# Rope on even and odd tiles, and a later place for its high and low halves, in the attention of a three-part layer

## What is computed

```python
def rotate_half(x):
    x1 = x[..., ::2]
    x2 = x[..., 1::2]
    return jnp.stack((-x2, x1), axis=-1).reshape(x.shape)

qkv = x @ Wqkv.T                     # x is layer-normalised before
q, k, v = split and turned to (b, head, t, 16)
q = cos * q + rotate_half(q) * sin   # angles: one frequency for each pair of features
k = cos * k + rotate_half(k) * sin
scores = q k^T / sqrt(16), causal
out = softmax(scores) v, heads side by side, @ Wo.T

x = x + 0.5 * ffn(layernorm(x))
x = x + attention(layernorm(x))
x = x + 0.5 * ffn(layernorm(x))
```

## Time and profile before

| | us |
|---|---|
| median of three timed runs | 2371.58 |
| their range | 2366.81 to 2373.09 |
| the profiled execution | 2371.06 |
| its span, from first to last instruction | 2369.3 |

### The profile page before, as it was taken

The page is one execution under the profiler, slowest core; times in us unless marked ns, Lnnn a source line. Parts: engine busy times, 40 slices in busy tenths (PEclk is TensorE's granted clock), DMA queues, the critical chain, the costliest instruction groups (busy, mean ns, idle before and its releaser), DMA issues. The chain is left out here.

```text
span 2369.3 us, 53760 instructions
## 1 busy us (share of the span) xinstructions
PE 2140.1 (90%) x18188; PEld 1161.5 (49%) x18188; DVE 1946.5 (82%) x4345; ACT 1358.6 (57%) x2567; POOL 1283.0 (54%) x1459
## 2 busy tenths in 40 slices
PE   2999999489999999999999999999999986999999
PEld 1666666324444444444444444444444433666666
DVE  4777777469999999998999899899899865777776
ACT  2555545136666676666666666666666663455444
POOL 3666666335545554554555455455455425666664
PEclk9999999779999999999999999999999997999999
DMA  4566666333454444444445444444444513666664
GB/s 157 179 201 202 202 207 198 94 63 88 93 97 90 91 101 98 91 95 86 91 98 100 91 90 98 89 100 95 89 90 97 93 37 126 201 203 199 201 201 165
DMA packets 280353, 295.33 MB, mean 125 GB/s; under 512 B 45744, under 2 KB 263184, under 8 KB 280080
## 3 DMA queue, kind: packets, MB, share of 16 engines
q1 hardware_dynamic: 279536, 290.85, 48.8%
q10 hardware_dynamic: 544, 1.05, 0.1%
HBM read 140.08 MB, written 83.89 MB: 95 GB/s over the span
## 5 line engine op out<-in xcount | busy, mean ns | idle before, releaser
L820 ACT ACTIVATE at_probs<-at_st_ps 128x512 f32<-128x512 f32 x1280 | 748.2, 604 | 473.7 <-PE at_st_ps L925 466.8
L753 DVE TENSOR_REDUCE at_mx<-at_mx_ps 128x1 f32<-128x512 f32 (+3 forms) x1408 | 837.7, 633 | 125.9 <-PE at_mx_ps L907 124.7
L675 POOL TENSOR_SCALAR_AFFINE_SELECT at_probs<-at_probs 128x512 f32<-128x512 f32 x512 | 319.1, 635 | 677.9 <-ACT at_probs L820 673.9
L925 PE MATMUL at_st_ps<-at_q_stack,at_k_stack 49*128 49x512 f16 (+3 forms) x2048 | 459.8, 302 | 73.2 <-ACT at_probs L820 71.0
L902 PE MATMUL at_mx_ps<-at_k_stack,at_q_stack 48*128 48x512 f16 (+3 forms) x2048 | 494.1, 304 | 29.8 <-DVE at_mx L753 18.5
L431 ACT ACTIVATE f_h<-f_h_ps,f_b1s 128x512 f32<-128x512 f32 x256 | 175.9, 687 | 358.3 <-PE f_h_ps L473 347.2
L925 PEld LDWEIGHTS at_st_ps<-at_q_stack,at_k_stack 49*128 49x128 f16 x2048 | 135.9, 94 | 460.4 <-ACT at_probs L820 339.8
L907 PE MATMUL at_mx_ps<-mask,turn 64*128 64x128 bf16 (+2 forms) x1408 | 342.6, 244 | 0.0
L942 PE MATMUL at_pv_ps<-at_probs,at_v 128*32 128x512 f32 (+3 forms) x4096 | 329.8, 440 | 0.8 <-POOL at_probs L675 0.6
L489 PE MATMUL f_y_ps<-f_w2hi,f_hlo 128*128 128x256 f16 x1024 | 279.2, 273 | 0.0
L489 PE MATMUL f_y_ps<-f_w2lo,f_hhi 128*128 128x256 f16 x1024 | 279.2, 273 | 0.0
(11 more groups left out here) (117 smaller groups left out, 3921.9 us busy)
## 6 DMA issues: line engine op xcount, KB each, us to landing
at_q_stack<-qk_image SPq DMA_DIRECT2D x192, 128.0 KB, 4.5
at_k_stack<-qk_image SPq DMA_DIRECT2D x192, 128.0 KB, 4.8
f_x<-in_x SPq DMA_DIRECT2D x32, 512.0 KB, 5.6
f_w1hi<-w_hi SPq DMA_DIRECT2D x128, 128.0 KB, 2.4
f_w1lo<-w_lo SPq DMA_DIRECT2D x128, 128.0 KB, 2.1
f_b2s<-in_b SPq DMA_DIRECT2D x128, 128.0 KB, 3.8
f_w2hi<-w_hi SPq DMA_DIRECT2D x128, 128.0 KB, 4.2
f_w2lo<-w_lo SPq DMA_DIRECT2D x128, 128.0 KB, 4.3
```

The lines of the kernel that those rows point to most:

```text
L675: nc.gpsimd.affine_select(out=ap, in_=ap, compare_op=ALU.is_ge, fill=0.0, base=0, pattern=[[0, d] for d in dims] + [[1, P]], channel_multi ...
L753: nc.vector.tensor_reduce(o_ap, i_ap, AX_X, ALU.max).then_inc(max_done, 1)
L820: nc.scalar.activation(probs[:, c, :], st_ps[c % 2][:], ACT.Exp, scale=DH ** -0.5).then_inc(exp_done, 1)
L925: ins = nc.tensor.matmul(bank[:, col:col + T - q0], k_stack[ss.par][rows, j + ha, kt * P:(kt + 1) * P], q_stack[ss.par][rows, j + ha, q0:T ...
```

## The change

Rope works on even and odd features in tiles of their own. The columns of the q and k weights are reordered on the host: tile 0 of q holds the even feature of every pair, tile 1 the odd one, and so for k. The partner of a feature is then in the other tile at the same partition, and no shuffle is needed. `begin_rope` on DVE keeps the product with cos alone; ACT copies x_ps to SBUF (`rope_raw`, new, at n = 3 and 7 of slots 0 and 1); POOL multiplies each raw tile by sin (`rope_sin`, both of a slot behind mask 0) and makes the two sums behind mask 3 (`rope_sums`, one a difference). `rope_high` moves from n = 0 and 2 to n = 3 and 5, `rope_low` from n = 0 and 3 to n = 4 and 7, both in slots 1 and 2 as before. `read_stack` takes the rows in the new order. In `normalise_output` four products become one.

```diff
-                        img = image[2 * part + lo].rearrange("(j a r) n -> a r j n", a=2, r=DH)[par]
+                        img = image[2 * part + lo].rearrange("(r j a) n -> a r j n", a=2, r=DH)[par]
...
-            def rope(n, t):
+            def rope_sin(n, t):
                 idx = 4 * n.b + t
                 pool.wait_ge(rope_in, idx + 1)
-                nc.gpsimd.tensor_tensor(by_sin[t % 2][:], swapped[t % 2][:], sin_t[:], ALU.mult).then_inc(sin_done, 1)
-
-                wait(pool, qk_lo, idx - 1)
-                pool.wait_ge(sin_done, idx + 1)
-                nc.gpsimd.tensor_tensor(rotated[t % 2][:], by_cos[t % 2][:], by_sin[t % 2][:], ALU.add).then_inc(rope_done, 1)
+
+                wait(pool, rope_done, 4 * n.b + t // 2 * 2)
+                nc.gpsimd.tensor_tensor(by_sin[t % 2][:], raw[t % 2][:], sin_t[:], ALU.mult).then_inc(sin_done, 1)
+
+            def rope_sums(n, u):
+                pool.wait_ge(sin_done, 4 * n.b + 2 * u + 2)
+                for e, op in ((0, ALU.subtract), (1, ALU.add)):
+
+                    wait(pool, qk_lo, 4 * n.b + 2 * u - 1 + e)
+                    nc.gpsimd.tensor_tensor(rotated[e][:], by_cos[e][:], by_sin[1 - e][:], op).then_inc(rope_done, 1)
...
                 if g < 2 and sample(s + 1):
-                    rope(s + 1, 2 * g)
+                    rope_sin(s + 1, 2 * g)
+                    rope_sin(s + 1, 2 * g + 1)
...
                 if g < 2 and sample(s + 1):
-                    rope(s + 1, 2 * g + 1)
+                    rope_sums(s + 1, g)
...
-                nc.vector.tensor_tensor(by_cos[t % 2][:], x_ps[t % 2][:], cos_t[:], ALU.mult)
-                nc.vector.stream_shuffle(swapped[t % 2][:], x_ps[t % 2][:], [i ^ 1 for i in range(32)]).then_inc(rope_in, 1)
+                nc.vector.tensor_tensor(by_cos[t % 2][:], x_ps[t % 2][:], cos_t[:], ALU.mult).then_inc(cos_done, 1)
...
-                for i in range(NT):
-                    ins = nc.vector.tensor_tensor(
-                        on[os.par][:, i, :].rearrange("p (j q d) -> p j q d", q=2, d=DH)[:, j:j + GH, half, :],
-                        turned[:, i, :, 0:DH],
-                        inverse[:, GH * i:GH * i + GH].rearrange("p (a d) -> p a d", d=1).broadcast_to([P, GH, DH]), ALU.mult)
-                ins.then_inc(on_done, 1)
+                nc.vector.tensor_tensor(
+                    on[os.par][:].rearrange("p i (j q d) -> p i j q d", q=2, d=DH)[:, :, j:j + GH, half, :],
+                    turned[:, :, :, 0:DH],
+                    inverse[:].rearrange("p (i a d) -> p i a d", i=NT, d=1).broadcast_to([P, NT, GH, DH]), ALU.mult).then_inc(on_done, 1)
...
-                    if g in (1, 2) and sample(s + 1) and n in (0, 3):
-                        rope_low(s + 1, 2 * (g - 1) + (n == 3))
+                    if g in (1, 2) and sample(s + 1) and n in (4, 7):
+                        rope_low(s + 1, 2 * (g - 1) + (n == 7))
...
+            def rope_raw(n, t):
+                idx = 4 * n.b + t
+                act.wait_ge(cos_done, idx + 1)
+
+                wait(act, sin_done, idx - 1)
+                nc.scalar.activation(raw[t % 2][:], x_ps[t % 2][:], ACT.Copy).then_inc(rope_in, 1)
...
-                    if g in (1, 2) and sample(s + 1) and n in (0, 2):
-                        rope_high(s + 1, 2 * (g - 1) + (n == 2))
+                    if g in (1, 2) and sample(s + 1) and n in (3, 5):
+                        rope_high(s + 1, 2 * (g - 1) + (n == 5))
+                    if g < 2 and sample(s + 1) and n in (3, 7):
+                        rope_raw(s + 1, 2 * g + (n == 7))
```

More of the change, by code:

```diff
@@ L528, in attention_phase @@
         xT = Split(sb("xThi", [P, NC, T], F16), sb("xTlo", [P, NC, T], F16))
-        swapped = [sb(f"swapped{i}", [P, T], F32) for i in range(2)]
+        raw = [sb(f"raw{i}", [P, T], F32) for i in range(2)]
         by_cos = [sb(f"by_cos{i}", [P, T], F32) for i in range(2)]
@@ L557, in attention_phase @@
         xT_lo, qk_done, rope_in, sin_done = sem("xT_lo"), sem("qk_done"), sem("rope_in"), sem("sin_done")
+        cos_done = sem("cos_done")
         rope_done, qk_hi, qk_lo, v_done = sem("rope_done"), sem("qk_hi"), sem("qk_lo"), sem("v_done")
@@ L1086 @@
     freqs = np.exp(np.float32(-np.log(10000.0)) * np.arange(0, DH, 2, dtype=np.float32) / np.float32(DH)).astype(np.float32)
-    angles = np.arange(T, dtype=np.float32)[None, :] * freqs[(np.arange(P) % DH) // 2][:, None]
-    sign = np.where(np.arange(P) % 2 == 0, -1.0, 1.0).astype(np.float32)[:, None]
+    angles = np.arange(T, dtype=np.float32)[None, :] * freqs[np.arange(P) // H][:, None]
+    halves = np.arange(D).reshape(H, DH // 2, 2).transpose(2, 1, 0).reshape(-1)
+    columns = np.concatenate([halves, D + halves, 2 * D + np.arange(D)])
     ins = {
         "x": L0_attn_x,
-        "WqkvT": np.asarray(L0_attn_Wqkv).T,
+        "WqkvT": np.asarray(L0_attn_Wqkv).T[:, columns],
         "WoT": np.asarray(L0_attn_Wo).T,
@@ L1099 @@
         "cos": np.cos(angles).astype(np.float32),
-        "sin": (np.sin(angles) * sign).astype(np.float32),
+        "sin": np.sin(angles).astype(np.float32),
     }
```

## The result

The changed kernel takes 2408.25 us (median of four runs, 2404.97 to 2414.14), the one before 2372.34 us (four runs, 2366.81 to 2381.37). The ratio is 1.0148 with a 95% interval from 1.0125 to 1.0171, so it is slower by 1.5%. The prediction was 2403 us.

The account below looks back on a forecast made before the run. PE's in-order queue was taken as the bound, DVE and ACT mattering only where PE waits. 0.41 + 0.92 + 0.33 - 0.60 = 1.06 us lost in each of 30 samples, on 2371, gave 2403 us; range 2365 to 2425.

Parts of the forecast that it names:

- ACT ahead of o32: Slots 0 and 1, n = 3: new ACT instructions ahead of o32 delay PE's turn_output by 0.41 and 0.92 us.
- Rival B: n = 3 to 5 of slots 0 to 2: PE turns no later, only the 0.61 us gain remains; 2352 us, chance 0.10.
- C: One instruction's delay reaches PE in slot 1, slot 2 loses nothing: 0.26 us for each sample, 2379 us; chance 0.08.
- rival A: DVE is the bound: 3.3 us come off each of 31 samples, 2269 us; chance 0.06.
- rival D: A mask or a stack comes late: 0.5 to 1 us more for each sample, 2418 to 2434 us; chance 0.08.
- DVE's saved work: Slot 1, n = 10: PE's wait for DVE ends, gaining 0.6 us for each sample.
- next late there is maximum 8: Slot 1, rope_low(1) between reductions 7 and 8: in time if it takes 0.6 us, 0.05 to 0.4 late if 1.2.
- Slot 2 on ACT: Slot 2: one more rope_high ahead of o32, one between exp(5) and exp(6); loss 0.33 us, or 0.17.
- GpSimd and the masks: Second sine product ahead of masks 1 to 3: slack of about 1 us, so it costs nothing.
- the low end: DVE's gain of only 0.2 us for each sample, by the skill's contention rule the likelier, some 6 to 12 us in all.
- The transfers: Later image writes and stack reads in new row order: costed at nothing, up to 1 us per sample if reads slow.
- The first sample: Its rope runs before any attention, in a chain through all engines: between -1 and +2 us once, taken as 0.

Follow-up runs that it names:

- no_shuffle: The kernel before without DVE's shuffle, GpSimd multiplying by_cos by sin instead, so neighbouring features aren't swapped: 2373.2 us, ratio 0.9984.
- copy_behind: The kernel before with one more unused 128 x 512 ACT copy in slots 0 and 1, right behind the copy to o32: 2379.8 us, ratio 1.0012.
- copy_ahead: The kernel before with one more unused 128 x 512 ACT copy at n = 3 of slots 0 and 1, ahead of o32: 2398.4 us, ratio 1.0086.
- slot2_dve: The changed kernel with slot 2's statistics at n = 2 instead of 1 and rope_low(3) at n = 8 instead of 7: 2408.1 us, ratio 1.0141.
- spread_aggr: The changed kernel with shorter statistics, rope_raw at n = 5 and 7, rope_high behind o32 and at 6, rope_low at 4 and 9 - g: 2377.3 us.
- respread: The changed kernel with statistics at n = 2, rope_raw at 5 and 7, rope_high at 5 and 9 - g, rope_low at 6 and 10 - g: 2423.5 us.
- read_order: The kernel before, reading the stack's rows in the changed kernel's order, which mixes the heads' features: 2377.1 us, ratio 1.0007.
- both_behind: The changed kernel with rope_raw and rope_high of n = 3 both behind the copy to o32: 2387.0 us, ratio 1.0044.

## Why the prediction was right

*The bound.* PE's queue sets the pace, and the other engines matter where PE waits for them: right. no_shuffle and copy_behind show it from both sides; neither 2.5 us less on DVE nor 1 us more on ACT changes the sample by more than 0.08 us.

*ACT ahead of o32.* Slot 0 was put at 0.41 us and measured 0.43. Slot 1 was put at 0.92; o32 came 1.00 us later behind exp(3), and PE 0.94. The wait at n = 8 absorbed none of it, as argued: slot 1 was still 1.33 us late there. copy_ahead and copy_behind show that the place is the cause. Rival B, which had ACT's queue not reach PE, and C are excluded by the 0.36 and 0.87 us of wait; rival A by no_shuffle. Of rival D nothing is seen in the steady samples: PE never waits for a mask there, and for a stack only at the first two samples.

*DVE's saved work.* This term was mis-sized. The wait at n = 10 did go (0.62 us, and 0.17 behind it), and rope_low(1) between reductions 7 and 8 cost nothing. But I followed DVE only to the end of slot 1. In slot 2 the statistics, stretched by GpSimd's sums, held up reduction 2 (0.28 us), and rope_low(3), stretched beside two masks, held up reduction 8 (0.43 us). The step that said "next late there is maximum 8" looked at the next wait of the same slot; the next late thing stood 6 us on, in a wait that no view counts as idle. The gain of 0.6 us was in fact 0.79 - 0.28 - 0.43 = 0.08. The term went wrong between "the wait of 0.61 us ends" and "a gain of 0.6 us for each sample".

*Slot 2 on ACT.* Put at 0.33, it shows as 0.08 in the sum, but slot2_dve shows a wait for o32 of 0.38 us as soon as reduction 2 is in time. So ACT's delay was there, about as large as forecast, and lay hidden behind DVE's. The place was another one, o32 and not exp(6). The 0.36 us between n = 4 and n = 8 of slot 2 belong to both engines: as the runs above show, either alone makes them.

*The sum.* By the table it is 0.43 + 0.94 + 0.08 - 0.08 - 0.04 (slot 1's beginning) = 1.33 us where 1.06 was forecast: slots 0 and 1 of ACT as forecast, 0.25 less for its slot 2, 0.52 less for DVE's gain. Two terms were wrong, in opposite directions, so that the total is near is in part luck: with DVE's gain alone corrected the sum would be 1.58 us, and 2418 us in all. 30 samples gave 36.3 us and not 31.8, and the total came out 5 us above the forecast, within the range.

*GpSimd and the masks.* PE never waited for a mask, as forecast: mask 3 of slot 0 ended 0.7 us ahead of the probs_v that needs it. But they held up DVE, and that was weighed for rope_low(1) alone, where it cost nothing (0.68 us, while the sine product behind it took 1.48 us in place of 1.27), and not for the small sums of the statistics and for rope_low(3). The rule of the Trainium skill (SBUF — State Buffer, Who interferes with whom) that I had given the low end to applies there with the trace's numbers: a VectorE instruction with two SBUF inputs took 1.05 us for 0.15, and rope_low 1.17 us for 0.68 beside two masks, which grew as well, and 1.55 and 1.58 us beside a sine product (spread_aggr, respread).

*The transfers* cost nothing (read_order). *The first sample* was put between -1 and +2 us: the part up to its first reduction took 2.9 us more, the sample itself 4.1 us less, at another granted clock for a part of it, so the term isn't shown.

*What would show it.* o32 waits of 0.4 and 0.9 us: seen. Slot 0 longer by 0.4, slot 1 by 0.3: 0.3 and 0.2, nearly so. Slot 2 by 0.3: 0.9, wrong. Slot 3 equal: 0.1 shorter. PE's waits for ACT larger by about 1.6 us in a sample: (71.9 + 37.3 - 68.4) / 30 = 1.36, less by what slot 2 doesn't show. DVE 3 us less busy in a sample: 1.9; 0.9 of the difference is the one stretched sum (L103).

## What to carry to other kernels

Of an in-order engine's queue the bounding engine pays for what stands ahead of the one instruction that it waits for, and not for what stands behind it, unless that runs into the next such instruction (both_behind). So a piece of new work wants the place where its engine is idle just before that instruction, not the place where its input is ready. Before a removed wait is booked as a gain, follow the bounding queue through the whole period and ask at each meeting point how late its partner already is, hidden waits too. When two engines are late at one point, as in slot 2 here, undoing either alone shows nothing, and only moving both shows what they cost together.

## What the runs showed of the hardware

A vector sum of four numbers for each partition, 0.15 us by itself, took 1.05 us and ended with GpSimd's pair of 128 x 512 sums, so a small instruction isn't safe there (after, slot 2). Two masks of GpSimd took 1.68 us in place of 1.22 beside a rope_low that took 1.17 in place of 0.68: both sides grew. With the same 1 KB pieces in another order of rows, an issue of SyncE took 0.60 us in place of 0.43, and the last of the six reads landed 0.40 us later (read_order, medians).
